# Attention weighted sums of a head pair in one group of 40 products instead of two groups of 20, with turned weights kept for two pairs and the output projection one step later

## The reference

```python
# B, S, H = 8, 512, 256; 16 heads of 64; cond_64 supplies one extra ("null") key and value
x = x + ternary_ffn(mixture_of_experts(x, cond_64, ...), ...)
y = attention(x, bias=fside_16xSxS_0, mask, g_in, null_bias, null_kv=cond_64, Wq, Wkv, Wo, g_out)
#   xn = layernorm(x, g_in);  q = 16 heads of xn @ Wq;  k, v = xn @ Wkv, shared by all heads
#   sim = q k^T + bias, causal and masked, and one null column;  attn = softmax(sim)
#   out = (attn @ v, heads side by side) @ Wo;  layernorm(out, g_out)
x = x + quantised_ffn(y, ...)
```

## Time and profile before

| | |
|---|---|
| median of 3 runs | 1398.55 us (1398.45 to 1400.82) |
| the profiled execution | 1398.35 us |
| its span, first to last instruction | 1396.6 us |
| mean granted TensorE clock | 0.962 of full speed |
| busy share TensorE / VectorE / ScalarE / GpSimd | 90% / 74% / 54% / 40% |
| one batch of the attention in the loop | 98.8 to 101.6 us |

### The profile page before, as it was taken

How to read it: one execution, slowest core, us unless ns; L and a number is a source line. 1 busy time by engine, 2 the same in 40 slices (tenths; PEclk the granted TensorE clock), 3 DMA queues, 4 the chain that set the end, 5 groups by cost and what they waited for, 6 DMA issues and landing times. The chain is left out here.

```text
span 1396.6 us, 29614 instructions
## 1 busy us (share of the span) xinstructions
PE 1256.0 (90%) x8710; PEld 1000.6 (72%) x8710; DVE 1039.0 (74%) x2792; ACT 757.2 (54%) x1942; POOL 565.0 (40%) x845
## 2 busy tenths in 40 slices
PE   3999999999886699999998999998999999986966
PEld 2768888888765578778777877887887788873323
DVE  5666676667644877787887887877878877886986
ACT  3223333333222567666765766766676677645643
POOL 1443323333322776354444444354453454531114
PEclk8999999999998899999999999999999999997986
DMA  6332122211201700001010000010010000202115
GB/s 231 108 99 77 65 72 106 91 61 61 91 1 53 262 12 2 1 2 32 2 32 3 2 31 2 1 32 3 2 32 1 2 16 2 78 1 65 45 61 180
DMA packets 49993, 70.57 MB, mean 51 GB/s; under 512 B 4466, under 2 KB 42611, under 8 KB 47796
## 3 DMA queue, kind: packets, MB, share of 16 engines
q1 hardware_dynamic: 49284, 68.55, 14.7%
q10 hardware_dynamic: 560, 0.20, 0.1%
HBM read 56.54 MB, written 12.19 MB: 49 GB/s over the span
## 5 line engine op out<-in xcount | busy, mean ns | idle before, releaser
L1082 POOL TENSOR_SCALAR scores<-scores,att_rinv 128x128 f32<-128x128 f32 (+3 forms) x512 | 266.9, 538 | 194.4 <-DVE att_rinv L1303 194.4
L1147 ACT ACTIVATE scores<-scores,att_top 128x128 f32<-128x128 f32 (+3 forms) x512 | 281.6, 553 | 88.6 <-DVE att_top L1285 88.1
L1285 DVE CUSTOM_DVE_ANT_0 scores<-ps_y,w_bias_b,w_null_s 128x128 f32<-128x128 f32 x448 | 229.3, 547 | 78.2 <-PE ps_y L1476 71.3
L301 POOL TENSOR_TENSOR act_w<-act_g,wide_w 128x512 f32<-128x512 f32 x64 | 105.8, 1653 | 283.2 <-DVE act_g L454 268.7
L1155 ACT ACTIVATE keep<-ps_up 128x128 f32<-128x128 f32 (+3 forms) x256 | 112.0, 438 | 167.4 <-PE ps_up L1487 164.1
L1487 PE MATMUL ps_up<-ident,scores 128*128 128x128 f32 x1280 | 191.2, 275 | 10.0 <-DVE keep L1313 9.4
L214 ACT ACTIVATE hid_hi<-hid 128x512 fp32r<-128x512 f32 x80 | 50.5, 632 | 245.2 <-DVE hid L472 245.2
L1487 PEld LDWEIGHTS ps_up<-ident,scores 128*128 128x128 f32 x1280 | 151.4, 141 | 31.2 <-issue 17.1
L1498 PE MATMUL ps_a<-keep,w_val 128*64 128x128 f32 x2560 | 169.1, 279 | 1.3 <-DVE keep L1313 1.3
L1498 PEld LDWEIGHTS ps_a<-keep,w_val 128*64 128x64 f32 x2560 | 138.1, 137 | 22.0 <-issue 20.0
L1564 PE MATMUL ps_gate<-w_wo,o_t 128*128 128x256 f32 x512 | 139.6, 392 | 0.0
(11 more groups left out here) (321 smaller groups left out, 2949.9 us busy)
## 6 DMA issues: line engine op xcount, KB each, us to landing
wide_w<-token_w_dram SPq DMA_DIRECT2D x16, 1024.0 KB, 4.6
x_raw<-in_x_t_dram SPq DMA_DIRECT2D x8, 512.0 KB, 3.8
x_nat<-in_x_nat_dram SPq DMA_DIRECT2D x8, 512.0 KB, 4.7
x_dram<-x_nat SPq DMA_DIRECT2D x8, 512.0 KB, 2.9
w_x1t<-x_dram SPq DMA_DIRECT2D x8, 512.0 KB, 4.1
x_tile<-x_dram SPq DMA_DIRECT2D x8, 512.0 KB, 4.4
out_dram<-res SPq DMA_DIRECT2D x8, 512.0 KB, 3.2
w_bias_b<-in_bias_dram SPq DMA_DIRECT2D x14, 256.0 KB, 4.1
```

The source lines that it names most:

```text
L301: nc.gpsimd.tensor_tensor(act_w[:, k % 2], act_g[:, k % 2], wide_w[:, k], ALU.mult).then_inc(sem.act_w_ready, 1)
L1082: nc.gpsimd.tensor_scalar(s, s, rinv[:, pp, q, hh:hh + 1], 0.0, ALU.mult, ALU.add).then_inc(sem.p_normed, 1)
L1147: nc.scalar.activation(s, s, ACT.Exp, scale=-1.0, bias=top[:, pp, q, hh:hh + 1], accum_out=lsum[:, pp, q, hh:hh + 1]).then_inc(sem.exp_don ...
L1285: dve.tensor_tensor_reduce(scores_of(pp, hh, q), psS[:, hh, 0:n], bias_of(w, h)[:, CAUSAL[q]:CAUSAL[q] + n], 1.0, null_s[:, par, q, h:h + ...
```

## The change

- `PLAG` goes from 8 to 10. `weighted` runs once a pair, at `i % 4 == 2`, over the pair's four steps: one group of 40 products where there were two of 20, at `i % 4 == 0` and `i % 4 == 2`. It waits for the copies of all four steps and signals `pv_done` once a pair.
- The turned weights are kept for two pairs: a second tile `turned_odd` of 128 x 2 x 2 x 640 float32 stands beside `w.turned_p`. The waits for `pv_done` are counted in pairs.
- The projection halves go from `i % 4 == 2, 3` to `i % 4 == 3` and `i % 4 == 0` of the next pair.
- `OUT`, `NORM_OUT`, `SCALE_OUT` and `LARGEST`, the steps of the last batch's output, each move one step later.
- After the last batch, the two remaining pairs' sums are formed in groups of 40 as well, and half 1 of the sixth pair's projection comes after the last of them.

```diff
-    TLAG, PLAG, NLAG = 6, 8, 5
+    TLAG, PLAG, NLAG = 6, 10, 5
...
-        pr = w.turned_p
+        pr = (w.turned_p, sb("turned_odd", [P, 2, 2, 5 * P]))
...
-            return pr[:, j // 2 % 2, hh, at:at + n]
-
-        def group(b, i, lag):
-            return STEPS // 2 * b + (i - lag) // 2
+            return pr[j // 4 % 2][:, j // 2 % 2, hh, at:at + n]
+
+        def pair(b, i, lag):
+            return PAIRS * b + (i - lag) // 4
...
-        OUT, SCALE_OUT, LARGEST = 12, (21, 22), (23, 24)
+        OUT, SCALE_OUT, LARGEST = 13, (22, 23), (24, 25)
...
-        NORM_OUT = (13, 14, 15, 16, 17, 18, 19, 20)
+        NORM_OUT = (14, 15, 16, 17, 18, 19, 20, 21)
...
-                    if j % 2 == 0 and not known(g, 2):
-                        act.wait_ge(sem.pv_done, g - 1)
+                    if j % 4 == 0 and not known(n, 2):
+                        act.wait_ge(sem.pv_done, n - 1)
...
                 def outputs_t(n, pp):
-                    act.wait_ge(sem.pv_done, 2 * n + 2)
+                    act.wait_ge(sem.pv_done, n + 1)
...
                 def weighted(J, j, par):
-                    pe.wait_ge(sem.pa_ready, J + 2)
-                    pe.wait_ge(sem.pb_ready, J + 2)
-                    for at in (j, j + 1):
+                    pe.wait_ge(sem.pa_ready, J + 4)
+                    pe.wait_ge(sem.pb_ready, J + 4)
+                    for at in range(j, j + 4):
...
                     late, J, j = lagged(b, i, PLAG)
-                    if i % 2 == 0 and (behind or not late):
+                    if i % 4 == 2 and (behind or not late):
                         if i == PLAG:
                             pe.wait_ge(sem.val_ready, b + 1)
-                        if j % 4 == 0 and (behind or i > PLAG):
+                        if behind or i > PLAG:
                             pe.wait_ge(sem.ot_ready, N + (i - PLAG) // 4)
                         weighted(J, j, 1 - par if late else par)
-                    if i % 4 >= 2 and (behind or p >= 3):
-                        before = b if p >= 3 else b - 1
-                        project(before, N + p - 3, (p - 3) % PAIRS, i % 4 - 2)
+                    if i % 4 == 3 and (behind or p >= 3):
+                        project(b if p >= 3 else b - 1, N + p - 3, (p - 3) % PAIRS, 0)
+                    if i % 4 == 0 and (behind or p >= 4):
+                        project(b if p >= 4 else b - 1, N + p - 4, (p - 4) % PAIRS, 1)
...
                     if j % 4 == 0:
                         pe.wait_ge(sem.ot_ready, N + (i - PLAG) // 4)
-                    if j % 2 == 0:
                         weighted(J, j, 1)
...
-                    if i in (2, 3):
-                        project(B - 1, N - 3, PAIRS - 3, i - 2)
+                    if i == 0:
+                        project(B - 1, N - 4, PAIRS - 4, 1)
+                    if i == 3:
+                        project(B - 1, N - 3, PAIRS - 3, 0)
+                project(B - 1, N - 3, PAIRS - 3, 1)
```

More of the change, by code:

```diff
@@ L1148, in exps, with turned_out @@
                                              accum_out=lsum[:, pp, q, hh:hh + 1]).then_inc(sem.exp_done, 1)
-                def turned_out(J, j, g):
-                    n = P * (ORDER[j % 4] + 1)
+                def turned_out(J, j, n):
+                    cols = P * (ORDER[j % 4] + 1)
                     act.wait_ge(sem.t_done, 2 * J + 1)
-                    if j % 2 == 0 and not known(g, 2):
-                        act.wait_ge(sem.pv_done, g - 1)
-                    nc.scalar.activation(turned_of(j, 0, 0, n), psT[:, 0, 0:n], ACT.Copy).then_inc(sem.pa_ready, 1)
+                    if j % 4 == 0 and not known(n, 2):
+                        act.wait_ge(sem.pv_done, n - 1)
+                    nc.scalar.activation(turned_of(j, 0, 0, cols), psT[:, 0, 0:cols], ACT.Copy).then_inc(sem.pa_ready, 1)
                 def null_exp(n, pp):
@@ L1223, in step @@
                     if behind or not late:
-                        turned_out(J, j, group(b, i, TLAG))
+                        turned_out(J, j, pair(b, i, TLAG))
                     exps(STEPS * b + i, i)
@@ L1255, in _ @@
                 nc.scalar.activation(w.squash[:], w.ffn.clip[:], ACT.Exp, scale=-1.0).then_inc(sem.clip_exp, 1)
-                for i in range(PLAG):
+                for i in range(2 * 4):
                     if i % 4 == 3:
@@ L1260, in _ @@
                         _, J, j = lagged(B, i, TLAG)
-                        turned_out(J, j, group(B, i, TLAG))
+                        turned_out(J, j, pair(B, i, TLAG))
                     if i == PNT + 1:
@@ L1306, in totals, with turned_out @@
                                             ).then_inc(sem.null_n_ready, 1)
-                def turned_out(J, j, g):
-                    n = P * (ORDER[j % 4] + 1)
+                def turned_out(J, j, n):
+                    cols = P * (ORDER[j % 4] + 1)
                     dve.wait_ge(sem.t_done, 2 * J + 2)
-                    if j % 2 == 0 and not known(g, 2):
-                        dve.wait_ge(sem.pv_done, g - 1)
-                    nc.vector.tensor_copy(turned_of(j, 1, 0, n), psT[:, 1, 0:n]).then_inc(sem.pb_ready, 1)
+                    if j % 4 == 0 and not known(n, 2):
+                        dve.wait_ge(sem.pv_done, n - 1)
+                    nc.vector.tensor_copy(turned_of(j, 1, 0, cols), psT[:, 1, 0:cols]).then_inc(sem.pb_ready, 1)
                 def null_weights_lo(b):
```

## The result

| | before | after |
|---|---|---|
| median | 1398.55 us (1398.18 to 1400.82, 5 runs) | **1392.14 us** (1390.93 to 1395.14, 5 runs) |
| ratio | | 0.9956, 95% interval 0.9941 to 0.9971 |
| profiled span | 1396.6 us | 1390.3 us |

The kernel is faster, by 6.4 us where 13.6 were forecast: right in direction and inside the range, with less than half of the size.

A forecast was written before the change was run, and what follows sets the result against it. TensorE and VectorE were taken to set the pace in turns. Loop batches -11.7, batch 0 -1.4, last batch -2.3 and end +1.8 gave -13.6 us, 1385.0 us forecast, range 1375 to 1393.

The forecast's parts named there:

- quiet pair: A pair without extra work, where TensorE has no waits: -0.34 us, the two gaps saved.
- list of signs: What the profile after would show, such as forty loads in 2.14 us and a pair 10.9 us long instead of 11.2.
- the second twenty are slower: Rival: in a run of 40 the added twenty loads cost more than 1.07 us; 1407 us, chance 0.07.
- no effect: Rival: the gaps move to other places, a pair gains nothing and the end costs 1.8; 1400 us, chance 0.05.
- The step that let `OUT` leave ScalarE's chain: Steps 12 and 13: the output copy leaves the chain that TensorE's queries wait for, so -0.90 us a batch.
- step 22 might grow by over 0.5: Sign of error: the prediction would be wrong if step 22 or 14 grew by more than 0.5 us.
- the saving of step 20: Loop batches, step 20: counted as nothing, because the moved last layernorm stage fills VectorE's 0.30 us idle at 22.
- batches 1 to 6: -11.7: Loop batches: step savings and costs sum to -1.95 us a batch, for six batches -11.7.
- Nothing hides these: +1.8: End of the kernel: 20 more products behind the last copy, +1.07 us, and a projection half, +0.73, both exposed.
- The last batch ... -2.3: Last batch, no input work: -0.34 x 8 = -2.7 us, with parts of steps 16, 18, 20 and 30 falling into waits.
- The same instructions one step later: Moved output copy and layernorm stages: the same instructions one step later, with nothing added to a DMA queue.
- VectorE takes most: Rival: moved output stages load VectorE, pairs 3 and 5 lose the saving and 0.3 us more each; 1391.8 us, chance 0.13.

The follow-up runs named there:

- experiment 2: Kernel before, with projection half 0 put between the two steps of the group at step 2 of a pair: 1411.79 us, ratio 1.0077.
- experiment 5: Changed kernel with no-operations or always-met waits added to VectorE's stream, some runs also with groups of 20 after the last batch: 1382.47 to 1391.81 us.
- experiment 4: Changed kernel with the output's copy, layernorm stages, scaling and maxima back at their old steps (`OUT` 12): 1390.68 us, ratio to before 0.9944.
- 5f: Changed kernel with groups of 20 after the last batch and two, four or six always-met waits ahead of VectorE's loop: 1386.46, 1385.23, 1382.47 us.
- experiment 3: Changed kernel with the projection halves back at steps 2 and 3 of a pair, the group of 40 alone: 1427.75 us, ratio to before 1.0201.
- experiment 1: Changed kernel with groups of 20 and the projection halves in their earlier order after the last batch: 1386.26 us, ratio to before 0.9913.

## Why the prediction was half right

**Right.** The quiet pair goes from 11.43 to 11.09 us, the -0.34 forecast (the lengths in the list of signs, 11.2 and 10.9, were both 0.2 short). The forty loads take 2.16 us (2.14 forecast), and the gaps ahead of the line are 41 with 8.2 us where the earlier trace rows had 112 with 20.0. The Trainium skill's pace of some 81 ns a pair (TensorE: Matmul & The Clock Gate, Back-to-back issue gap) does not show in a group of 40: 2.16 / 40 is 54 ns, as in the earlier trace rows. The rival "the second twenty are slower" is out, and "no effect" with it, since experiment 2 prices a pair of form changes at 0.35. Batch 0 came to its forecast by cancelling: pair 0, which has no weighted sums, took 0.9 us more and pair 3 1.15 less, and over the runs of experiment 5 that are set against the changed kernel the batch varies from 97.6 to 99.3 us. That is luck. The loop batches without a turn in front came to -1.7 to -2.5, -1.95 forecast, with errors inside that cancel: pair 2 gave -0.85 where -0.34 stood, pair 3 -0.8 where -0.59 stood, pair 0 -0.34 where -0.65 stood, pair 4 +0.12 where nothing stood. The step that let `OUT` leave ScalarE's chain was right: with `OUT` at 12 the 0.92 us wait is there, with 13 it is not (experiment 4). Step 17 took the shorter step 16 into its wait: 4.18 to 4.78 us. That step 22 might grow by over 0.5 was named as a sign of error, and it did, 3.0 to 3.8; the saving of step 20 (3.13 to 2.58 on average), which the working did not expect, paid for much of it, so that pair 5 came to +0.4 on average where +0.31 stood.

**Wrong, first: "batches 1 to 6: -11.7"**, measured -8.0. The steps were costed as if a batch were the same wherever it stands. Batches 3 and 5 lost their whole saving because VectorE's loop begins at a place in the code where its restart stops twice. The change did that by taking six instructions out of VectorE's stream ahead of the loop, an edit costed at nothing. Four or six other instructions in front take the second stop away again, shown in 5f. With six, batch 5 then has its saving (96.96 us against 98.79 before), and batch 3 has not (98.64 against 98.81), with the clock at 0.50 behind its turn. So the prediction's step lacked both what the start of VectorE's loop costs and a clock that can fall behind a turn; in the changed kernel the first of them decides.

**Wrong, second: "Nothing hides these: +1.8"** at the end, measured +4.7. The work behind the last copy was counted right, at full speed, and is 1.8 of the 3.6 us there. Forty products in one group wait for the last copy, so TensorE is idle in the short stretches ahead of it instead of working on twenty, and the clock then stood at 0.50: 40 loads in 3.22 us where 2.16 is the price at full clock, and 14 in 3.33 where 10 took 2.02 before and 4 more take 0.73. That is 1.6 more. The other 1.1 come ahead of the last copy, where the prediction counted nothing: the first group of 40 took 3.38 us, partly at the same low clock, and the transposes behind it start 13.2 us behind the last scores where they started 11.6 behind them. The earlier trace rows had one group at that level, 2.00 for 20; the prediction used it as a bound for a rival and not for the end, where it belonged.

**Wrong, third: "The last batch ... -2.3"**, measured -0.45. Two parts of it show. At step 5 TensorE is now early enough to meet the chain of the null weights, which the working did not look for in a batch without input work:

```profile
1151.42 0.19 PEld L34 LDWEIGHTS ps_a<-xn_hi,w_wq_hi 128*128 128x128 f32 x1 [0.61 <-DVE w_null_nt L1317]
```

And at steps 23 and 24 the scaling that moved with `SCALE_OUT` (L1095) now stands on GpSimd between the normalisations (L1082), one of which TensorE's transposes then wait for. Beside it a small instruction of VectorE grows:

```profile
1203.21 1.65 DVE L1293 TENSOR_TENSOR null_d<-att_top,w_null_s 128x8 f32<-128x8 f32 x1
1203.48 1.28 POOL L1095 TENSOR_TENSOR out_raw<-out_raw,w_g_out 128x512 f32<-128x512 f32 x1
...
1205.58 0.20 PEld L1487 LDWEIGHTS ps_up<-ident,scores 128*128 128x128 f32 x2 [1.25 <-POOL scores L1082]
```

L1293 takes 0.17 us in most other places. With the old steps the last batch is 1.36 shorter, 1.24 of it in pair 6 (experiment 4); what the queue on GpSimd and what the longer L1293 have of that is not separated. "The same instructions one step later" is what this failed on: at the new step they had another neighbour.

"VectorE takes most", whose time of 1391.8 is the nearest to the measured one, was not what happened: pairs 3 and 5 of the batches without a turn did not lose the saving. In sum: the errors are +3.7, +2.9 and +1.8, less the 1.0 us by which the attention started sooner, together 7.4, and the profiled spans differ from the forecast by 7.3 us.

## What to carry to other kernels

Look at the first step behind each loop turn on each engine. Here VectorE's idle time of several us there went with the packets of kind `instruction`, and an edit that added or removed a few instructions ahead of the loop doubled or halved it. Look at the granted clock there as well before a loss is given to one cause. Before a group of products is merged, ask what its first half did for the engine while it waited for the second: here the projection half that took its place covered VectorE (experiment 3), and at the end groups of 20 kept the clock up (experiment 1). And before an inserted instruction is taken for a test, count whether it is in the executed program.

## What the hardware showed that was not expected

- A turn of VectorE's loop costs 2.8 to 3.1 us from the branch to the first instruction, and in the runs with a second stop within the first instructions of the loop 2.2 to 3.0 more (5.57 against 2.76 us idle; 5.66, 2.81 and 2.90 with 2, 4 and 6 instructions in front). That this is code arriving in pieces is inferred from the place of the stops and the DMA records.
- TensorE has a stop of its own at each turn, 2.4 and 2.1 us before, 2.5 and 2.4 in the changed kernel. At some turns the granted clock is 0.50 behind it (4 loads in 1.40 us at 743.60, against 0.73 at the turn into batch 5, where it was 1.00).
- Spread instructions in VectorE's loop changed pair 5 of the odd batches by 0.9 us, and six waits ahead of the loop by 0.55, with no change of work. How is left open.
- A 128x8 operation of VectorE (L1293) took 1.61 to 1.66 us, in place of the usual 0.17, in each of the seven batches of the changed kernel in which it met a 128x512 one of GpSimd (L1095). It is not the only thing that lengthens it: in batch 0 of the kernel before it took up to 1.7 us without one.
